# A graph network kernel: waits folded into instructions in the maximum passes, and a slot's eight low one-hots made by one comparison of 1024 columns

## The reference

```python
x = _layernorm(x + L0(x))   # attention with 4 heads, softmax over each node's edges
x = _layernorm(x + L1(x))   # two layers with a segment maximum
x = _layernorm(x + L2(x))   # two layers with a segment mean
x = _layernorm(x + L3(x))   # three layers with a weighted segment sum
```

```python
msg = x[src] @ W_msg + edge_attr @ W_edge
agg = jax.ops.segment_max(msg, dst, num_segments=x.shape[0])
agg = jnp.where(jnp.isneginf(agg), 0.0, agg)
return agg + x @ W_root + b
```

## Time and profile before

| | us |
|---|---|
| median of three runs | 8198.6 |
| lowest and highest of the three | 8197.04, 8199.33 |
| span of the profiled execution | 9645.8 |
| attention pass in that span, 195 slots | 2211.9 |
| first and second maximum pass in that span, 195 slots each | 2502.7, 2494.8 |

### The profile page before, as it was taken

One profiled execution on the slowest core, in us unless ns is written; L12 is line 12 of the kernel. 1 busy time (PEld: TensorE's weight loads), 2 busy tenths in 40 slices (PEclk: granted clock), 3 DMA queues, 4 the chain that ended last, 5 costly groups with the idle time before them and its releaser, 6 DMA issues.

```text
span 9645.8 us, 76664 instructions
## 1 busy us (share of the span) xinstructions
PE 4165.1 (43%) x19184; PEld 2488.9 (26%) x19184; DVE 5483.9 (57%) x13228; ACT 1494.5 (15%) x2140; POOL 4860.8 (50%) x5030
## 2 busy tenths in 40 slices
PE   1100000000344444444443444444444438999999
PEld 1000000000311111111111111111111118899999
DVE  4554444444467667676775677677777757422222
ACT  0222222222211111111111111111111110010000
POOL 6676666666265556655664656556666640000000
PEclk6555555555565555555555555555555559999999
DMA  4232222222033333333332333333333325567667
GB/s 131 72 88 74 78 76 76 73 79 74 25 106 103 102 103 107 102 104 102 106 104 70 104 104 104 103 103 107 105 104 104 105 69 209 210 235 263 234 233 250
DMA packets 642351, 1133.27 MB, mean 117 GB/s; under 512 B 164861, under 2 KB 422288, under 8 KB 641635
## 3 DMA queue, kind: packets, MB, share of 16 engines
q1 hardware_dynamic: 360256, 440.38, 14.6%
q0 software_dynamic: 159184, 251.10, 12.6%
q10 hardware_dynamic: 122578, 438.40, 11.4%
HBM read 716.67 MB, written 412.70 MB: 117 GB/s over the span
## 4 chain that ended last, share of the span: by engine, by line
DVE 43%; PE 17%; another core or an unknown queue 16%; issue 13%; POOL 8%; ACT 1%; DMA 1%; DVEq 0%; SPq 0%; POOLq 0%; ACTq 0%
DVE BUF L1498 8%; DVE BUF L1490 7%; POOL CG L446 7%; DVE BUF L1489 5%; PE psB L722 5%; PE psX L722 5%; PE psA L722 5%; DVE STG L1514 3%; DVE XTQ L1514 3%; DVE XTQ L1523 3%; DVE STG L1523 3%; PE psO L664 1%; DVE EX L1437 1%; DVE terms L1435 1%
## 5 line engine op out<-in xcount | busy, mean ns | idle before, releaser
L446 POOL DMA_INDIRECT CG<-table,BUF x4704 | 4519.4, 961 | 2924.2 <-issue 1385.3
L692 PE MATMUL psO<-WE,BUF 128*128 128x384 f32 x1568 | 1118.7, 868 | 186.9 <-DMA BUF<-in_edge_attr 141.5
L1490 DVE TENSOR_SCALAR BUF<-iota,EG 128x392 bf16<-128x392 f16 x3136 | 1010.3, 322 | 106.7 <-issue 105.8
L1489 DVE TENSOR_SCALAR BUF<-iota,EG 128x128 bf16<-128x128 f16 x3136 | 848.9, 271 | 52.2 <-issue 33.5
L952 ACT COPY psX<-BUF 128x384 f32<-128x384 f32 x392 | 189.0, 482 | 4246.5 <-DVE XTQ L1523 1635.7
L765 PE MATMUL psA<-ident,F 128*100 128x128 f32 x1 | 0.5, 455 | 1940.6 <-DVEq L1403 1940.6
L472 POOL CAST CG<-EG x35 | 27.9, 796 | 1356.2 <-DVEq L1173 1356.2
L1523 DVE TENSOR_TENSOR_SCAN XTQ<-psX,XTQ 128x432 f32<-128x432 f32 x392 | 392.7, 1043 | 454.0 <-remote 404.6
L1523 DVE TENSOR_TENSOR_SCAN STG<-psX,STG 128x432 f32<-128x432 f32 x392 | 392.8, 1044 | 442.1 <-remote 370.4
L692 PEld LDWEIGHTS psO<-WE,BUF 128*128 128x128 f32 x1568 | 480.5, 327 | 628.9 <-issue 326.5
L701 PE MATMUL psB<-BUF 128*128 128x392 bf16 x523 | 251.7, 481 | 856.0 <-remote 349.5
(11 more groups left out here) (276 smaller groups left out, 6651.5 us busy)
## 6 DMA issues: line engine op xcount, KB each, us to landing
BUF<-counts SPq DMA_DIRECT2D x245, 784.0 KB
BUF<-counts ACTq DMA_DIRECT2D x245, 784.0 KB
counts<-BUF SPq DMA_DIRECT2D x1572, 98.0 KB
hist<-CG ACTq DMA_DIRECT2D x392, 384.0 KB
hist<-CG ACTq DMA_DIRECT2D x196, 416.0 KB
CG<-table,BUF POOLq DMA_INDIRECT x4704
BUF<-in_edge_attr SPq DMA_DIRECT2D x392, 128.0 KB
table<-TB SPq DMA_DIRECT2D x14, 336.0 KB
```

The costliest lines, as they stand in the source:

```text
L446: pool.indirect_dma_start(out=rows_in[:, u % RING, k, :], out_offset=None, in_=tab, in_offset=bass.IndirectOffsetOnAxis(ap=SRC[:, u * S + ...
L692: mm = pe.matmul(ETERM[:, s, a, 0:4 * DIM], EA[:, s, a, :], WE[:, m, :, :].rearrange("k c d -> k (c d)"), start=True, stop=True)
L1489: ts(LO[:, j, a, :], iota16[:, 0:P], STEP[:, 2 + a, n:n + 1], None, ALU.is_equal)
L1490: hot = ts(RHS[:, j, a, :], iota16[:, :], STEP[:, a, n:n + 1], None, ALU.is_equal)
```

## The change

In the maximum passes:

- DVE makes all eight low one-hots of a slot (4 steps, 2 each) with one `tensor_tensor` comparison of 1024 columns at the slot's start, in place of eight `tensor_scalar` comparisons of 128 columns.
- The waits for `acc_ready` and `counted`, which stood in front of each accumulation, stand now in front of the two high one-hots of the same step. The copy of the last column stands after the slot's first step. The waits in front of the scans stand in front of the addition.
- PE no longer waits for `eterm_used` and `acc_ready`.
- SP loads the four row numbers of a slot at once and writes with byte addresses. The row numbers are multiplied by the bytes of a row beforehand (`last_rows`, once).

```diff
             def flush(u):
+                _, starts_at = nc.values_load_multi_w_load_instructions(ADDR[0:1, u * CS:(u + 1) * CS], [mybir.EngineType.SP])
                 for j in range(CS):
-                    k = u * CS + j
-                    sp.wait_ge(acc_ready, m * HALF + k + 3)
-                    row = sp.value_load(ADDR[0:1, k:k + 1])
-                    sp.dma_start(counts16[bass.ds(row, P, BG), :], ACC[:, j, :]).then_inc(flushed[j], 16)
+                    sp.wait_ge(acc_ready, m * HALF + u * CS + j + 3)
+                    sp.dma_start(bass.AP(bytes16, starts_at[j], [[BG * ROW_BYTES, P], [1, ROW_BYTES]]),
+                                 ACC[:, j, :].bitcast(U8)).then_inc(flushed[j], 16)
...
                 pe.wait_ge(ea_loaded[s], 16 * (m * ITERS + u // 2 + 1))
-                pe.wait_ge(eterm_used, m * SLOTS + u + 1)
...
                     pe.wait_ge(onehot_ready, k + 1)
-                    if k >= 3:
-                        pe.wait_ge(acc_ready, k)
...
             link(tt(row, row, ROW_F, ALU.add))
+            link(ts(row, row, float(ROW_BYTES), None, ALU.mult))
...
             def one_hots(n):
-                j = n % CS
-                for a in range(2):
-                    ts(LO[:, j, a, :], iota16[:, 0:P], STEP[:, 2 + a, n:n + 1], None, ALU.is_equal)
-                    hot = ts(RHS[:, j, a, :], iota16[:, :], STEP[:, a, n:n + 1], None, ALU.is_equal)
-                hot.then_inc(onehot_ready, 1)
+                j, k = n % CS, m * HALF + n - 2
+                if n >= 2:
+                    dve.wait_ge(acc_ready, k + 2)
+                ts(RHS[:, j, 0, :], iota16[:, :], STEP[:, 0, n:n + 1], None, ALU.is_equal)
+                if n >= 2:
+                    dve.wait_ge(counted, k + 2)
+                ts(RHS[:, j, 1, :], iota16[:, :], STEP[:, 1, n:n + 1], None, ALU.is_equal).then_inc(onehot_ready, 1)
 
             def accumulate(n):
                 dve.wait_ge(flushed[j], 16 * (k // CS + 1))
-                dve.wait_ge(counted, k + 2)
-                dve.wait_ge(acc_ready, k + 2)
...
+                if u:
+                    dve.wait_ge(counted, m * HALF + u * CS + 1)
+                tt(LO, iota16[:, 0:P].unsqueeze(1).unsqueeze(1).broadcast_to([P, CS, 2, P]),
+                   STEP[:, 2:4, u * CS:(u + 1) * CS].rearrange("p a j -> p j a").unsqueeze(3).broadcast_to([P, CS, 2, P]), ALU.is_equal)
                 for j in range(CS):
                     one_hots(u * CS + j)
                     if u * CS + j >= 2:
                         accumulate(u * CS + j - 2)
-                if u:
-                    dve.wait_ge(scanned, q * SLOTS + u)
-                step(nc.vector.tensor_copy(max_cols[b][:, :, 0:1], max_cols[1 - b][:, :, S:K9]))
-                dve.wait_ge(gathered[r], 16 * S * (q * LAPS + u // RING + 1))
-                dve.wait_ge(eterm_ready[s], m * ITERS + i + 1)
+                    if j == 0:
+                        if u:
+                            dve.wait_ge(scanned, q * SLOTS + u)
+                        step(nc.vector.tensor_copy(max_cols[b][:, :, 0:1], max_cols[1 - b][:, :, S:K9]))
                 if u >= 2:
                     dve.wait_ge(block_done[(u - 2) % RING], q * LAPS + (u - 2) // RING + 1)
+                dve.wait_ge(dve_step, steps[0])
+                dve.wait_ge(resets_ready, q * SLOTS + u + 1)
+                dve.wait_ge(eterm_ready[s], m * ITERS + i + 1)
+                dve.wait_ge(gathered[r], 16 * S * (q * LAPS + u // RING + 1))
...
-                dve.wait_ge(resets_ready, q * SLOTS + u + 1)
-                dve.wait_ge(dve_step, steps[0])
-                dve.wait_ge(eterm_used, m * SLOTS + u + 3)
+                dve.wait_ge(eterm_used, m * SLOTS + u + 1)
```

More of the change, by code:

```diff
@@ L43 @@
 TRASH = NB * P * BG
+ROW_BYTES = 2 * CW
 CH = 392
@@ L59 @@
 F16 = mybir.dt.float16
+U8 = mybir.dt.uint8
 ALU = mybir.AluOpType
@@ L396, in build @@
     blocks16 = counts16[0:NB * P * BG, :].rearrange("(b p g) c -> b p (g c)", p=P, g=BG)
+    bytes16, halves32 = counts16.bitcast(U8).tensor, counts.bitcast(BF16).tensor
     blocks32 = counts[0:NB * P * BG, :].rearrange("(b p g) c -> b p (g c)", p=P, g=BG)
@@ L615, in _ @@
                     sp.sem_inc(turn["sp"], 1)
-                    row = sp.value_load(ADDR[0:1, bass.ds(k, 1)], min_val=0, max_val=TRASH + BG - 1)
-                    sp.dma_start(counts[bass.ds(row, P, BG), :], ACC32).then_inc(again_flushed, 16)
+                    start = sp.value_load(ADDR[0:1, bass.ds(k, 1)], min_val=0, max_val=(TRASH + BG - 1) * ROW_BYTES)
+                    sp.dma_start(bass.AP(halves32, start, [[BG * ROW_BYTES, P], [1, ROW_BYTES]]),
+                                 ACC32.bitcast(BF16)).then_inc(again_flushed, 16)
             sp.wait_ge(again_flushed, 16 * STEPS + 16)
@@ L1157, in _ @@
         dve.sem_inc(out_used, 1)
-        dve.sem_inc(eterm_used, 2)
         dve.sem_inc(block_seen, 3)
@@ L1526, in running_pass @@
             for n in range(HALF - 2, HALF):
+                dve.wait_ge(acc_ready, m * HALF + n + 2)
+                dve.wait_ge(counted, m * HALF + n + 2)
                 accumulate(n)
```

## The result

The changed kernel takes 8244.3 us (median of 4 runs, 8238.1 to 8248.4); the kernel before, beside it on the same chip, 8199.0 us (4 runs, 8197.0 to 8202.6). The ratio is **1.0053, 95% interval 1.0042 to 1.0065**: slower by 45 us, where 255 us were forecast. Run again beside the kernel before it gave 1.0059 (1.0042 to 1.0076). The direction was right; the size was not.

A forecast was written before the change was run, and what follows sets the result against it. GpSimd's gathers were taken to bound all three passes; the comparison's hold-up of 0.65 us in each of 392 slots adds 255 us to 8198.6, giving 8454 us. Its own range was 8297 to 8571, the overall range 8198 to 8600.

The forecast's parts named there:

- The gathers bound all passes: All three passes: GpSimd's eight gathers a slot set the time, with DVE about 0.9 us a slot below.
- A gather every 1.23 us, 9.85 us a slot: All 585 slots: pace without a profile, from the 8198.6 us median less 2436 us for the rest.
- 2436 us for all the rest: Outside the three passes: what the profiled span of 9645.8 us leaves after the passes' 7209 us.
- VectorE's slot stays at 8.97 us: Maximum passes: DVE's changes of -1.30, +1.15, +0.24 and -0.09 us sum to 0.00; slot between 8.8 and 9.7 us.
- The comparison at 1.22 us: Slot of a maximum pass: length of the new 1024-column comparison, 1.07 + 0.15 us, judged from L1233.
- A comparison with two operands in SBUF holds up a gather that starts inside it, for 1.07 us: Maximum passes, once a slot: a gather starting in the comparison's reading time waits for what is left of it.
- The 1.10 us that the forecast gave to a hold over the whole instruction: Fifth gather's loss by the skill page's rule instead of 0.95 us, 59 us more over 392 slots.
- The phase: Maximum passes: rows used 2.5 us after the last gather's start, window 6.0 to 7.1, fifth gather at 6.15 loses 0.95 us.
- if the landing is 0.2 us later ... the loss is near 0: Maximum passes: with a later landing or faster gathers, the fifth gather slips by before the comparison's window.
- The narrow one-hots give 0.07 us for three gathers back: Maximum passes: gathers no longer held by narrow one-hots regain 0.07 us each, at most three a slot.
- SyncE's part is worth nothing: SP's one register load and no bounds step for four flushes: no gain without a profile, a lot in the trace.
- rival 1: Maximum passes: the hold-up misses, or is hidden because DVE's 8.97 us is the bound; 8200 to 8260 us, chance 0.14.

The follow-up runs named there:

- the first four experiments: Low one-hots one by one (9503.7 us), comparison alone (9500.7), SyncE's part alone (9715.8), comparison moved later by a memset (9511.9), each beside the kernel before at 9838 us.
- The small stores: Changed kernel with the store of a slot's rows cut from 96 to 16 columns in the second maximum pass: 8333.9 us, ratio 1.0148.

## Why the prediction was wrong, point by point

- **The gathers bound all passes**: right, by the chain and by seven gathers (8.96 us a slot then, 10.25 us with eight).
- **A gather every 1.23 us, 9.85 us a slot**: off. It is 1.25 us and 10.0 us before holds, 10.17 us with them. I had trusted 2436 us for all the rest, from a trace with pauses; without them it is 8242.4 - 1961 (attention) - 1995 - 1997 = 2289 us. That the earlier trace rows were an effect of the profiler was wrong too: beside the first four experiments runs without a profile took as long, though the time judged had indeed no such pauses in it.
- **VectorE's slot stays at 8.97 us**: right, 8.96 us. The comparison at 1.22 us: 1.20. Its cost is hidden, and so is that of the folded waits (0.9994 without the comparison).
- **A comparison with two operands in SBUF holds up a gather that starts inside it, for 1.07 us**: right. 0.55 us lost from 0.47 us in, 0.93 us lost from 0.15 us in. The Trainium skill, page "SBUF — State Buffer", section "SBUF: two separate sides", has the lock on the shared port pair last for the whole instruction of 1.20 us and lets whichever starts first block the other fully; here a gather 0.26 us ahead leaves the comparison at 1.20 us, and one 0.99 us in loses only 0.08 us, not 0.21. The hold ends 1.06 us after the comparison's start, close to the forecast's reading time of 1.07 us. The measurement decides. The 1.10 us that the forecast gave to a hold over the whole instruction was a little off: with the comparison from 5.9 to 7.1 us a gather at 6.15 us would lose 1.0 us. The forecast's sum at this place was a little off: it started the window 0.08 us late and so ended it at 1.15 us, which makes 0.95 us of loss where 1.06 us would make 0.8.
- **The phase: the step that failed.** "Its rows are used 2.5 us after that gather's start" came from the attention pass, where it is 2.53 us in the new trace too, and was carried to the maximum passes, where it is 3.2 us. That put the window at 6.0 to 7.1 us, over the fifth gather; it lies at 6.6 to 7.7 us, between the fifth (6.38) and the sixth (7.63). The comparison costs 0.10 to 0.11 us a slot, not 0.65: some 41 us instead of 255. The trace of the kernel before could not have given the landing in a maximum pass: with its pauses the gathers ran far ahead there, and a slot's rows were used some 30 us after its last gather. The forecast named this edge ("if the landing is 0.2 us later ... the loss is near 0") and still gave it 0.14. That the loss is as small as that is luck of phase: the landing was 0.7 us later and not 0.2, and at the forecast's pace of 1.23 us the sixth gather would have started at 7.4 us, into the last 0.3 us of the window. The small stores and the missing SyncE part show how steep it is.
- **The narrow one-hots give 0.07 us for three gathers back**: hardly. What is held outside the comparison went from 0.17 to 0.14 us a slot, since the 392-column ones are what holds and they stay.
- **SyncE's part is worth nothing**: wrong in kind. By itself 1.0018; with the comparison it saves some 45 us, and the landing moves with it.
- **The range** (8198 to 8600) holds 8244, but in the part that rival 1 had been given (8200 to 8260), not in the forecast's own (8297 to 8571). Of rival 1 it is the branch in which the gather slips by; VectorE is not the bound.

## What to carry to other kernels

Where GpSimd's software DMAs bound a stage, count what VectorE's instructions do to them, not what they do to VectorE: a comparison with two SBUF operands is a window in which no gather gets going, and where it stands against the gathers is worth more than its duration. A phase must be read in the very stage in which it counts, from a trace whose span fits the time that is judged, and an edit whose gain or loss flips within 0.2 us of phase should be forecast as two cases of like weight, not as one. The parts of such a change don't add (1.0125, 1.0010 and 1.0018 alone, 1.0053 together); none of the versions tried that does all the work beats the kernel before by more than the measurement can tell. And an inserted idle instruction tests something only if the trace shows that it has moved the others.

## What the runs showed of the hardware

- With a VectorE comparison of 1024 columns that reads two SBUF operands, a gather loses what is left of 1.06 us from the comparison's start: 0.99 us in, 0.08 us lost; 0.47 in, 0.55; 0.15 in, 0.93. A gather that started 0.1 us or more ahead of it is not held up, nor is the comparison.
- A memset of 400 fp32 columns (0.39 us) holds gathers that start under it as well, and the comparison right behind it holds them on: ten gathers lose 1.1 to 1.4 us in the two passes.
- Comparisons against one scalar with 392 columns hold gathers up by 0.04 to 0.10 us mostly, 99% of them by at most 0.12 us in the changed kernel; in the kernel with the comparison alone 308 gathers at an accumulation's start lose 0.26 us, for a reason that is open. Scans and the addition, each with an operand in PSUM, don't: over 340 gathers under scans in the first maximum pass, mean loss below 0.01 us.
- Fewer bytes to store made the kernel 76 us slower, idle work of 0.39 us a slot some 170 us slower. A memset of 8 columns (0.07 us) in each of 1568 steps vanished beside a one-hot: the steps kept their 1.12 us.
- The kernel before ran at 8199 to 8215 us (medians) and, beside the first four experiments, at 9838 us. SyncE's part alone ran at 8217 to 8227 us eight times and at 9375 and 10759 us twice, so the long times can come and go between executions of one program.
